# The second MLP product of a windowed-attention kernel as three fp16 products

## The reference, cut to what matters

```python
h = shift_token(x)
q, k, v = split(h @ wqkv)                  # 8 heads of 64
q, k = rotary_xpos(l2norm(q) * qs, l2norm(k) * ksc)
x = x + local_attention(q, k, v) @ wo      # windows of 128, each sees itself and the one before
h = layernorm(shift_token(x)) * lg + lb
a, g = split(h @ w1 + b1)                  # 2 x 682 columns
x = x + (a * gelu(g)) @ w2 + b2            # the product of this change
```

## Time and profile before

| | |
|---|---|
| median of 3 runs | 3179.91 us (3177.46 to 3179.95) |
| the profiled execution | 3178.97 us, its span 3177.2 us |
| TensorE busy | 2982.5 us, 94% |
| VectorE busy | 2656.8 us, 84% |
| ScalarE busy | 1847.9 us, 58% |
| GpSimd busy | 1754.4 us, 55% |

### The profile page before, as it was taken

One profiled execution on the slowest core, in us unless ns is written; L12 is line 12 of the kernel. 1 busy time (PEld: TensorE's weight loads), 2 busy tenths in 40 slices (PEclk: granted clock), 3 DMA queues, 4 the chain that ended last, 5 costly groups with the idle time before them and its releaser, 6 DMA issues.

```text
span 3177.2 us, 79721 instructions
## 1 busy us (share of the span) xinstructions
PE 2982.5 (94%) x24952; PEld 2581.8 (81%) x24952; DVE 2656.8 (84%) x7754; ACT 1847.9 (58%) x4226; POOL 1754.4 (55%) x2083
## 2 busy tenths in 40 slices
PE   6898989783899999999999999999999999999997
PEld 3676767573688888888888888888888888888886
DVE  6878788755788888888888888899998999999895
ACT  4233241402566666666666666666676676676673
POOL 1231314024566666666666666676676676676773
PEclk9999999995899999999999999999999999999999
DMA  1120202025111111111111111222112212122221
GB/s 38 38 70 28 80 14 87 4 83 205 33 50 49 53 51 49 52 48 49 54 50 50 50 48 50 56 56 60 56 55 57 65 55 60 55 55 60 63 56 46
DMA packets 273326, 177.65 MB, mean 56 GB/s; under 512 B 95758, under 2 KB 271090, under 8 KB 272754
## 3 DMA queue, kind: packets, MB, share of 16 engines
q1 hardware_dynamic: 273138, 175.50, 19.0%
HBM read 104.08 MB, written 54.54 MB: 50 GB/s over the span
## 4 chain that ended last, share of the span: by engine, by line
PE 72%; POOL 1%; issue 1%; DVE 0%; DMA 0%; ACT 0%; POOLq 0%; SPq 0%; DVEq 0%; ACTq 0%
PE b_ps L824 17%; PE b_ps L899 14%; PE b_ps L910 10%; PE b_ps L852 8%; PE b_ps L840 7%; PE b_ps L878 6%; PE b_ps L865 6%; PE b_ps L809 2%; PE b_ps L802 2%; PE b_ps L791 1%; POOL b_sq L1145 0%; POOL b_rn L1178 0%; POOL b_t L1167 0%; POOL b_kr L1183 0%; DVE b_probs L1093 0%
## 5 line engine op out<-in xcount | busy, mean ns | idle before, releaser
L957 ACT ACTIVATE b_probs<-b_probs,b_negmax 128x256 f32<-128x256 f32 x1024 | 506.0, 496 | 78.3 <-DVE b_negmax L1093 77.5
L824 PE MATMUL b_ps<-b_wqkv,b_hT_hi 128*128 128x512 f32 x1536 | 493.0, 402 | 1.0 <-DVE b_hT_lo L981 1.0
L899 PE MATMUL b_ps<-b_h2T,b_w 128*128 128x256 f16 x4224 | 473.0, 273 | 6.5 <-DMA b_h2T<-b_xh_hl 6.4
L899 PEld LDWEIGHTS b_ps<-b_h2T,b_w 128*128 128x128 f16 x4224 | 413.6, 98 | 55.1 <-DMA b_h2T<-b_xh_hl 6.8
L1145 POOL TENSOR_TENSOR b_sq<-b_sq 128x512 f32<-128x512 f32 (+5 forms) x768 | 419.3, 546 | 62.4 <-ACT b_sq L938 22.3
L1178 POOL TENSOR_TENSOR b_rn<-b_ss_min,b_mhalf 128x16 f32<-128x16 f32 x128 | 377.2, 2947 | 108.9 <-DVE b_ss_min L1005 108.7
L1106 DVE TENSOR_SCALAR b_probs<-b_probs,b_rinv 128x256 f32<-128x256 f32 x1024 | 409.6, 442 | 18.2
L1155 POOL TENSOR_TENSOR b_rstd<-b_var,b_mhalf 128x1 f32<-128x1 f32 x128 | 72.2, 564 | 552.3 <-DVE b_var L1066 552.3
L407 PE MATMUL a_ps<-a_xn_hl,a_E 128*128 128x256 f16 x3072 | 352.5, 277 | 18.9 <-DVE a_E L290 18.9
L407 PEld LDWEIGHTS a_ps<-a_xn_hl,a_E 128*128 128x128 f16 x3072 | 303.3, 99 | 58.5 <-issue 19.9
L910 PE MATMUL b_ps<-b_w,b_hid 128*128 128x256 f32 x1536 | 342.2, 379 | 1.2 <-DVE b_hid L1129 1.2
(11 more groups left out here) (137 smaller groups left out, 6191.6 us busy)
## 6 DMA issues: line engine op xcount, KB each, us to landing
b_hx<-xs_dram SPq DMA_DIRECT2D x256, 64.0 KB, 1.9
b_rot<-rot_dram SPq DMA_DIRECT2D x128, 128.0 KB, 2.1
b_xr<-xs_dram SPq DMA_DIRECT2D x128, 128.0 KB, 2.1
xp_dram<-b_xp SPq DMA_DIRECT2D x128, 128.0 KB, 1.7
b_h<-xp_dram SPq DMA_DIRECT2D x256, 64.0 KB, 1.8
a_x_res<-in_L_attn_x_dram SPq DMA_DIRECT2D x64, 128.0 KB, 2.2
x_dram<-a_x SPq DMA_DIRECT2D x64, 128.0 KB, 1.7
xs_dram<-a_xo SPq DMA_DIRECT2D x64, 128.0 KB, 1.8
```

Source lines behind the costliest of these rows:

```text
L824: last = nc.tensor.matmul(ps[:, bank, :], hT[:, k, :], wqkv[:, ds(layer(s), 1), part, k, bank * INNER:(bank + 1) * INNER], start=(k == 0 a ...
L899: last = nc.tensor.matmul(ps[:, bank, half * 2 * P:(half + 1) * 2 * P], w1[:, ds(layer(2 * j), 1), wp, k, first:first + P], h2T[:, hp, k, ...
L957: nc.scalar.activation(probs[:, h, :], probs[:, h, :], ACT.Exp, bias=negmax[:, h:h + 1], scale=-1.0, accum_out=rowsum[:, h:h + 1]).then_in ...
```

## The change

The hidden values and `w2` are each scaled by a power of two per layer and split into two fp16 halves. The second product becomes three fp16 products per chunk (36 of 128x128 by 256 columns for a pair of windows, where there were 12 in fp32). The scale of `w2` is found as that of `w1`; the scale of the hidden values (`hid_scale`) is found in the setup from the largest weights and biases; `xpp` takes the scale out again (`out_unit`). The high halves are made by ScalarE and the low halves by VectorE, in three pieces of two chunks each (128 x 512 numbers), in the odd slot: ScalarE's before the squares of q, before those of k and before the copy of v; VectorE's after the rotation of q, before and after the rotation of k. In the setup the maximum over the partitions now covers `w1`, `w2` and the first biases, and VectorE's subtractions for `wqkv` and `wo` stand before it in VectorE's program.

```diff
-        w2 = sb("w2", [P, LAYERS, HC, D])
+        w2 = sb("w2", [P, LAYERS, 2, HC, D], F16)
+        hid_scale, out_unit = sb("hid_scale", [P, LAYERS]), sb("out_unit", [P, LAYERS])
...
-            hid = sb("hid", [P, HC, 2 * P])
+            hid, hid_hl = sb("hid", [P, HC, 2 * P]), sb("hid_hl", [P, 2, HC, 2 * P], F16)
...
# setup, GpSimd
-                        pool.wait_ge(top_ready, LAYERS)
+                        pool.wait_ge(top_ready, 3 * LAYERS)
                         nc.gpsimd.partition_all_reduce(top_all[:], top[:], P, RED_MAX).then_inc(top_shared, 1)
# setup, ScalarE
-                    nc.scalar.activation(w2[:, l], w2[:, l], ACT.Copy, scale=w1_unit[:, l:l + 1])
+                    nc.scalar.activation(w2[:, l, 0], w2_f[:, l], ACT.Copy, scale=w2_scale[:, l:l + 1]).then_inc(w2_hi, 1)
# setup, VectorE
+                dve.wait_ge(loaded, 16 * DMAS)
+                for l in range(LAYERS):
+                    nc.vector.tensor_reduce(top[:, 1, l:l + 1], w2_f[:, l].rearrange("p c n -> p (c n)"), AX.X, ALU.max, apply_absolute_value=True).then_inc(top_ready, 1)
...
+                for l in range(LAYERS):
+                    dve.wait_ge(w2_hi, l + 1)
+                    nc.vector.scalar_tensor_tensor(w2[:, l, 1], w2_f[:, l], w2_scale[:, l:l + 1], w2[:, l, 0], ALU.mult, ALU.subtract)
# slots, TensorE, end of the odd slot
-                        pe.wait_ge(hid_ready, HC * (j + 1))
+                        pe.wait_ge(hid_lo, HID_PIECES * (j + 1))
...
                         for n in range(2):
                             for c in range(HC):
-                                last = nc.tensor.matmul(ps[:, 3, n * D:(n + 1) * D], hid[:, c, n * P:(n + 1) * P], w2[:, ds(layer(2 * j), 1), c, :],
-                                                        start=(c == 0), stop=(c == HC - 1))
+                                for a, (hp, wp) in enumerate(PARTS):
+                                    last = nc.tensor.matmul(ps[:, 3, n * D:(n + 1) * D], hid_hl[:, hp, c, n * P:(n + 1) * P],
+                                                            w2[:, ds(layer(2 * j), 1), wp, c, :],
+                                                            start=(c == 0 and a == 0), stop=(c == HC - 1 and a == 2))
# slots, ScalarE; called as hid_high(0) before the squares of q, (1) before those of k, (2) before the copy of v
+                def hid_high(piece, r, pairs, layer):
+                    j = pairs - 2
+                    if r % 2 == 1 and in_range(2 * j):
+                        chunks = slice(2 * piece, 2 * piece + 2)
+                        act.wait_ge(hid_ready, HC * j + chunks.stop)
+                        wait(act, w2_done, j)
+                        nc.scalar.activation(hid_hl[:, 0, chunks, :], hid[:, chunks, :], ACT.Copy, scale=hid_scale[:, ds(layer(2 * j), 1)]).then_inc(hid_hi, 1)
# slots, VectorE
+                def hid_low(piece, r, pairs, layer):
+                    j = pairs - 2
+                    if r % 2 == 1 and in_range(2 * j):
+                        chunks = slice(2 * piece, 2 * piece + 2)
+                        dve.wait_ge(hid_hi, HID_PIECES * j + piece + 1)
+                        nc.vector.scalar_tensor_tensor(hid_hl[:, 1, chunks, :], hid[:, chunks, :], hid_scale[:, ds(layer(2 * j), 1)], hid_hl[:, 0, chunks, :],
+                                                       ALU.mult, ALU.subtract).then_inc(hid_lo, 1)
...
                     rotate(s, r, 0, q_sq, q_terms, qr_ready)
+                    hid_low(0, r, pairs, layer)
...
                         nc.vector.tensor_copy(xh_hl[:, 0, :], xh[:]).then_inc(xh_hi, 1)
+                    hid_low(1, r, pairs, layer)
                     rotate(s, r, 1, k_sq, k_terms, kr_ready)
+                    hid_low(2, r, pairs, layer)
                     output_stats(pairs - 3, r, layer)
                     oT_low(s - 2)
```

More of the change, by code:

```diff
@@ L50 @@
 NT = LAYERS * NW
+HID_TOP, PRE_FLOOR = 2.0 ** 15, 2.0 ** -50
+HID_PIECES = HC // 2
 BLOCKS_PER_BATCH = WPB + 1
@@ L618, in _ @@
-                dve.wait_ge(step, 4)
-                nc.vector.tensor_scalar(w1_scale[:], pow2_inv[:], W1_TOP, None, ALU.mult).then_inc(scale_ready, 1)
-                for l in range(LAYERS):
-                    dve.wait_ge(qkv_hi, l + 1)
-                    nc.vector.tensor_tensor(wqkv[:, l, 1], wqkv_f[:, l], wqkv[:, l, 0], ALU.subtract)
+                nc.vector.tensor_scalar(w1_unit[:], pow2[:, 0], 1.0 / W1_TOP, None, ALU.mult).then_inc(step, 1)
+                nc.vector.tensor_scalar(w2_unit[:], pow2[:, 1], 1.0 / W1_TOP, None, ALU.mult).then_inc(step, 1)
@@ new lines, in _ @@
+                dve.wait_ge(step, 7)
+                nc.vector.tensor_scalar(pre_pow2[:].bitcast(I32), pre_floor[:].bitcast(I32), 0x7F800000, None, ALU.bitwise_and).then_inc(step, 1)
+                dve.wait_ge(step, 8)
+                nc.vector.scalar_tensor_tensor(pre_sq[:], pre_pow2[:], 4.0, pre_pow2[:], ALU.mult, ALU.mult).then_inc(step, 1)
+                dve.wait_ge(step, 9)
+                nc.vector.reciprocal(pre_inv[:], pre_sq[:]).then_inc(step, 1)
+                nc.vector.tensor_scalar(pre_half[:], pre_sq[:], 1.0 / HID_TOP, None, ALU.mult).then_inc(step, 1)
@@ L932, in run @@
                         nc.scalar.copy(kT[:, :, par * P:(par + 1) * P], by_pair(ps[:, 6, :])).then_inc(kT_hi, 1)
+                    hid_high(0, r, pairs, layer)
                     if in_range(s):
@@ L936, in run @@
                         nc.scalar.activation(sq[:, 0:HEADS, :], by_head(ps[:, 0, :]), ACT.Square).then_inc(q_sq, 1)
+                    hid_high(1, r, pairs, layer)
+                    if in_range(s):
                         act.wait_ge(k_done, s + 1)
                         nc.scalar.activation(sq[:, HEADS:2 * HEADS, :], by_head(ps[:, 1, :]), ACT.Square).then_inc(k_sq, 1)
+                    hid_high(2, r, pairs, layer)
+                    if in_range(s):
                         act.wait_ge(v_done, s + 1)
@@ L947, in run @@
                             nc.scalar.copy(probsT[:, p, :], ps[:, 3 + p, :]).then_inc(pT_kept, 1)
+                    if in_range(t):
                         act.wait_ge(pv_done, t + 1)
@@ L1124, in run @@
                     if r % 2 == 0 and in_range(2 * j):
-                        wait(dve, w2_done, j)
+                        wait(dve, hid_hi, HID_PIECES * j)
                         for c, bank in enumerate(W1_BANKS):
```

65 lines of the change are left out of this document (44 added, 21 removed).

## The result

The changed kernel takes 3306.28 us (median of 4 runs, 3306.16 to 3306.62); the kernel before took 3179.28 us (4 runs). The ratio is 1.0401, 95% interval 1.0383 to 1.0419: slower by 127 us, where I had forecast 69 and had ended my range at 3290. The profiled spans are 3304.5 and 3177.2 us, 127.3 us apart.

A forecast was written before the change was run, and what follows sets the result against it. The prediction took TensorE's own work as the loop's bound, with VectorE next. From 3178.97 us it added 10 (setup), 6.6 (layer 0), 49.3 (layer 1) and 3 (end): 3247.9, so 3248 us; range 3182 to 3290 us.

The forecast's parts named there:

- The odd slot of layer 1: Loop, layer 1: low halves make oT_low 2.57 us late, slot 1.7 us longer; 29 x 1.7 = 49.3 us.
- The rule of the Trainium skill: Odd slots and setup: a two-SBUF-input Vector instruction and a GpSimd instruction reading SBUF exclude each other; the second blocks.
- the clock falls: Rival, odd slots of layer 1: the 2.3 us stand lowers TensorE's clock, 29 x 2 = 58 us more, 3306 us; chance 0.06.
- The even slots: Loop: TensorE is their bound; VectorE's extra 0.9 us lateness fits its 3.4 us idle per pair, so no added time.
- The odd slot of layer 0: Loop, layer 0: oT_low 1.1 us late, slot 0.2 us longer; 33 x 0.2 = 6.6 us.
- the 0.99 us: Odd slot of layer 1: slack between kr's end at 2531.60 and TensorE's transposes of it at 2532.59, before the change.
- Setup and end: Setup +10 us, from the later common-scale reduction and waits for GpSimd; end +3 us, from unhidden halves and slot 127.
- the third rival: Losses and gains meet: layer 0 gains 30 us, layer 1 loses 23, setup costs 8; 3180 us, no change; chance 0.06.

The follow-up runs named there:

- the reductions: The changed kernel with each low half replaced by a maximum over the same 512 columns, result unused, low halves left zero: 3264.80 us, ratio 1.0265.
- The late kernel before: The kernel before with four tensor_reduce of 512 columns added on VectorE in each odd slot, ahead of output statistics and oT_low: 3305.38 us, ratio 1.0394.

## Why the prediction failed

**The odd slot of layer 1: right, 1.7 us forecast, 1.76 measured** where the clock stays whole (19.04 against 17.28; 0.08 of it is the shift of the tiles, which I had not in the sum). Each step holds in kind: the low halves 1.31, 0.75 and 1.16 us (forecast 0.96 with the wait for GpSimd, 0.55 and 1.24), `oT_low` 2.53 us late (2.57; that it is no later though the low halves sum to 0.47 us more is luck), a stand of 1.9 to 2.5 us at `wo`, mostly 2.2 (2.3), and of 0.53 at `kr` (0.6), the product 3.93 us from L949 to L840 (3.93). 28 x 1.76 = 49.3 us. The rule of the Trainium skill that the prediction used (SBUF — State Buffer, Who interferes with whom) agrees with these low halves. The same section says that `tensor_reduce` never contends with GpSimd on this chip, and that `tensor_scalar` can enter a mode that does: the reductions took 0.67 to 0.69 us, all 192 of them, and the addition of EPS, a `tensor_scalar`, 1.28 us beside GpSimd's 1.26.

**The clock: the step that failed first.** I gave the rival "the clock falls" 0.06, because TensorE would still be busy over 90% of the pair. It was (467.92 of 500 us), and the fall still came in 16 of 28 odd slots of layer 1, 1.03 us each: 16.5 us. The busy share of a pair said nothing about it; the stand of some 2.3 us in the middle did, and the earlier trace rows had shown me such a fall behind 2.6 us of idle time in 4. The late kernel before shows that the stand does it without the change. The rival's price of 2 us in every slot was too high by its two factors, and its 3306 us equal the measured time by chance.

**The even slots: the step that cost most.** I wrote that the even slot doesn't give it back and costs nothing, since VectorE's idle time of 3.4 us per pair lies in it. It costs 0.55 us in layer 0 and 0.28 us in layer 1: 31 x 0.55 + 28 x 0.28 = 25 us. The idle time was misread twice. Of the 3.4 us of a pair in layer 1 the trace before has 2.21 in the even slot and 1.15 in the odd one, and in every second even slot 1.2 of it is the stand at the turn of the loop, marked "issue" (1.2 to 1.9 us after the change, in both layers). The turn is most of the cost: 20.43 against 19.43 us for the slots that open one in layer 0, and 19.45 for all with the loops written out. 0.08 us of each slot is the shift of the tiles by 16 bytes; some 0.1 us stays unexplained.

The turn alone doesn't cost this. The late kernel before has the same stands of VectorE at the turns of layer 0 (1.6 to 2.0 us), and its even slots are no longer than before. There VectorE is hardly later than TensorE itself (`oT_low` 1.1 us late and the slot 0.96 longer, 2.2 and 2.1 in layer 1); in the changed kernel it is 0.7 and 0.8 us later (1.19 against 0.49, 2.53 against 1.76). So the turn seems to cost where VectorE enters the even slot later than TensorE does; no run varies this by itself, and why VectorE doesn't stand at the turns of layer 1 in the kernels with no low half and with one is open.

**The odd slot of layer 0: right in kind, mis-sized.** Forecast 0.2 us, measured 0.49. `oT_low` is 1.2 us late, not 1.1, and the transposes of `kr` had less slack than the 0.99 us that I read from one slot of layer 1: from the mean starts of `kr` (15.41 of 17.27 us, and 1.04 to run) it is 0.8. The shift of the tiles adds 0.08. 31 x 0.29 = 9 us.

**Setup and end.** The first load of the loop is issued at 785.66 us instead of 774.38: 11.3, forecast 10. The order was not as forecast in one place (timeline of the setup, GpSimd, VectorE and SyncE's issue, answering to the earlier trace rows):

```profile
765.17 8.81 POOL L578 TENSOR_TENSOR p_rot_all<-p_rot_all,p_head_scale 128x4096 f32<-128x4096 f32 x1 [6.79 <-issue]
...
765.34 8.68 DVE L657 TENSOR_SCALAR p_pre_half<-p_pre_sq 128x2 f32<-128x2 f32 x1
...
774.20 6.21 DVE L665 SCALAR_TENSOR_TENSOR b_w<-p_w_f,p_w_scale,b_w 128x2816 f16<-128x2816 f32 x2
...
785.66 0.34 SPq L761 DMA_DIRECT2D b_hx<-xs_dram  x1
```

What GpSimd's product blocked was a multiplication of two numbers per partition, 8.68 us long, and the low halves of `w1` behind it took their plain 3.1 us each. The end costs 8 us instead of 3.

In sum: of the 58 us missed, 25 are the even slots, 16.5 the clock, 9 the odd slots of layer 0, 5 the end and 2.6 the setup and the filling. What the end's 5 us are made of I have not taken apart. One slip moved nothing: the range that began at 3182 us left out the third rival (3180) too, which I didn't say.

## What to carry to other kernels

When work is put on an engine that others wait for, don't only ask whether it has idle time: ask what that idle time is (a stand marked "issue" at a loop's turn is no reserve), and list all that stands behind the new work up to the next place where the bound engine waits. A saving on the bound engine is worth no more than the slack of the next in line: 0.58 of 1.25 us here, and the low halves cost 1.1 to 2.9 us in the same slot. Between two engines that block each other, one long instruction at a place where the other is idle beat three short ones here (1.80 against 3.22 us), and taking away one that is blocked handed the wait to the next. A busy share over a whole pair doesn't tell whether the clock falls; look for single stands, and for two in a row.
